# An adaptive layernorm and a mixture of eight experts on one core: the routing of a pair moved one slot back, its rows scattered one block per slot, and the first experts' bounds, rows and register reads moved forward

## What is computed

```python
z = relu(x @ Wd[ids] + bd[ids])                       # 256 -> 128, adapter of the sequence
y = x + z @ Wu[ids] + bu[ids]
y = layernorm(y) * g[ids] + b[ids]

probs = softmax(y @ gate_w + gate_b)                  # 8 experts
values, chosen = top_k(probs, k=2)
values = values / (sum(values) + 1e-9)
moe = sum over e of weight[e] * (gelu(y @ ew1[e] + eb1[e]) @ ew2[e] + eb2[e])
out = x + y + gelu(y @ sh_w1 + sh_b1) @ sh_w2 + sh_b2 + moe     # 256 -> 1024 -> 256
```

## Time and profile before

| | |
|---|---|
| runs of the kernel before | 699.71, 700.79, 702.68 us; median 700.79 |
| the profiled execution | 698.72 us, of which 697.0 is the span of the core's instructions |
| PE, DVE, ACT, POOL busy | 616.9, 510.9, 388.1, 386.5 us of the span |
| mean granted PE clock | 0.96 |
| phase one | to about 277.5 us |
| full expert tiles | 283.2 to about 633 us |
| half expert tiles and the end | 633 to 697 us |

### The profile page before, as it was taken

How to read it: one execution, slowest core, us unless ns; L and a number is a source line. 1 busy time by engine, 2 the same in 40 slices (tenths; PEclk the granted TensorE clock), 3 DMA queues, 4 the chain that set the end, 5 groups by cost and what they waited for, 6 DMA issues and landing times.

```text
span 697.0 us, 16951 instructions
## 1 busy us (share of the span) xinstructions
PE 616.9 (89%) x5073; PEld 491.0 (70%) x5073; DVE 510.9 (73%) x1198; ACT 388.1 (56%) x662; POOL 386.5 (55%) x320
## 2 busy tenths in 40 slices
PE   4465988887987898799999999999999999999894
PEld 2232655564654465688888888888888888888673
DVE  2859679575767567369898989889897776776652
ACT  1536655366375575457667666777664354354442
POOL 2434765657557441015666666575666766766534
PEclk9878999999999999899999999999999999999998
DMA  8754464636313364634756666655724424424310
GB/s 278 254 136 114 139 185 119 181 108 198 101 34 111 92 214 138 196 79 100 143 132 146 131 135 134 123 123 115 152 42 78 69 47 69 65 38 62 60 28 3
DMA packets 116742, 81.33 MB, mean 117 GB/s; under 512 B 71090, under 2 KB 106162, under 8 KB 116658
## 3 DMA queue, kind: packets, MB, share of 16 engines
q1 hardware_dynamic: 101346, 61.16, 34.7%
q0 software_dynamic: 13296, 16.92, 12.8%
q10 hardware_dynamic: 2016, 2.16, 1.0%
HBM read 43.21 MB, written 24.42 MB: 97 GB/s over the span
## 4 chain that ended last, share of the span: by engine, by line
PE 65%; DVE 10%; ACT 6%; DMA 6%; issue 5%; SPq 5%; another core or an unknown queue 2%; POOLq 0%; ACTq 0%; POOL 0%; DVEq 0%
PE H L1196 28%; PE Y L1212 26%; SPq L282 4%; PE H L1144 4%; DMA xT<-wreg 4%; PE Y L1156 3%; PE Z L1086 2%; ACT wreg L499 2%; DVE wreg L762 1%; DVE wreg L788 1%; ACT hf L552 1%; ACT hh L560 1%; DMA wreg<-in_wpack 1%; DVE wreg L731 1%
## 5 line engine op out<-in xcount | busy, mean ns | idle before, releaser
L1196 PE MATMUL H<-xT,wreg 128*128 128x256 f16 (+1 forms) x1872 | 206.9, 265 | 9.7 <-DMA xT<-xs_rows 5.7
L1196 PEld LDWEIGHTS H<-xT,wreg 128*128 x1872 | 173.9, 98 | 35.9 <-issue 12.1
L1212 PE MATMUL Y<-wreg,hh 128*128 x1136 | 188.3, 273 | 0.0
L1212 PE MATMUL Y<-wreg,hl 128*128 x568 | 154.8, 273 | 0.0
L601 ACT ACTIVATE hf<-H,prme 128x256 f32<-128x256 f32 (+1 forms) x312 | 145.7, 547 | 1.4 <-ACT prme L592 0.2
L1017 DVE SCALAR_TENSOR_TENSOR hl<-hf,prme,hh 128x512 f16<-128x512 f32 (+1 forms) x156 | 130.2, 835 | 5.5
L1015 DVE TENSOR_SCALAR hh<-hf,prme 128x512 f16<-128x512 f32 (+1 forms) x156 | 82.2, 527 | 70.0 <-ACT hf L601 69.3
L455 POOL TENSOR_SCALAR b2w<-b2t,wsel 128x256 f32<-128x256 f32 x71 | 79.2, 1252 | 87.7 <-DVE wsel L1032 87.7
L1212 PEld LDWEIGHTS Y<-wreg,hh 128*128 128x128 f16 x1136 | 111.1, 98 | 14.0
L1144 PE MATMUL H<-xT,wreg 128*128 128x512 f16 x384 | 99.5, 414 | 8.2 <-DMA xT<-wreg 7.8
L1156 PE MATMUL Y<-wreg,hh 128*128 128x256 f16 x512 | 85.6, 273 | 7.0 <-DVE hl L960 6.1
(11 more groups left out here) (189 smaller groups left out, 712.4 us busy)
## 6 DMA issues: line engine op xcount, KB each, us to landing
stage<-in_w SPq DMA_DIRECT2D x16, 1024.0 KB
b2t<-in_b SPq DMA_DIRECT2D x39, 128.0 KB
wreg<-in_wpack SPq DMA_DIRECT2D x16, 256.5 KB
wreg<-in_xt SPq DMA_DIRECT2D x16, 256.0 KB
wreg<-in_x SPq DMA_DIRECT2D x16, 256.0 KB, 5.6
wreg<-in_vecs SPq DMA_DIRECT2D x16, 256.0 KB, 3.5
out_y<-wreg SPq DMA_DIRECT2D x16, 256.0 KB
xs_rows<-wreg SPq DMA_DIRECT2D x9, 260.0 KB
```

Source lines behind the costliest of these rows:

```text
L1196: m = pe.matmul(H[c][:, half * w:(half + 1) * w], we[:, bass.ds(e + h * 2048 + k * 1024 + col, P)], xp[:, a + k, 0:w], start=i == 0, stop= ...
L1212: m = pe.matmul(Y[n % 2][:, j * D:(j + 1) * D], hx[:, n % 2, c * w + j * P:c * w + (j + 1) * P], we[:, bass.ds(e + 4096 + h * 2048 + c * D ...
```

## The change

The change touches the tables of slots, and the places of seven steps:

- `then(s, o)` is `at` with one slot more for pairs 0 to 5. `logits`, `choose`, `exps`, `rank`, `place` and `weigh` use it: offsets 8, 9, 9, 10, 11 and 11 in place of 7, 8, 8, 9, 10 and 10. Pairs 6 and 7 stay.
- `scatter(p, i)` of pairs 0 to 5 stands at the end of slot offset 11 + i, one block (two DMAs) per slot. For pairs 6 and 7 two blocks stand in slots 10 and 11 as before.
- The pads move from slot 26 to 28, and `load_rows(0)` and `(1)` from slot 30 to 29, ahead of the output stores of slot 30.
- The first expert's units: `unit_sums(3)` goes to slot 27, `unit_bound(2)` and `(3)` between `gemm1` and `gemm2` of slots 28 and 29, `unit_high` and `unit_low` of both one slot forward.
- PE reads `ready` and `slot` of tile 0 between slots 30 and 31, and those of tile n+1 between `expert_gemm1(n)` and `expert_gemm2(n-1)`. From tile 32 on `ready` is not read, and the wait is for all units.
- ACT reads its register and copies its parameters before it waits for PE; `first_bias(n)` stands in tile n itself, behind group 2.
- DVE's `select(n)` stands ahead of tile n's `split_h`.

```diff
+def then(s, o):
+    return [p for p in range(NP) if s - base(p) == o + (p < NP - 2)]
-START = [-6, -2, 27, 28]
+START = [-6, -2, 27, 27]
 # sync engine
+                if s == 29:
+                    sp.wait_ge(v_etab, 1)
+                    for n in range(2):
+                        load_rows(n)
-                if s == 26:
+                if s == 28:
                     sp.wait_ge(v_ptab, 1)
                     for e in range(NE):
                         pad(e)
-                if s == 27:
-                    sp.wait_ge(v_etab, 1)
-                if s == 30:
-                    for n in range(2):
-                        load_rows(n)
 # gpsimd
-                for p in at(s, 11):
-                    scatter(p, 2)
-                    scatter(p, 3)
...
-                for p in at(s, 10):
-                    scatter(p, 0)
-                    scatter(p, 1)
+                for p in range(NP):
+                    for i in range(4):
+                        if s == base(p) + (11 + i if p < NP - 2 else 10 + i // 2):
+                            scatter(p, i)
 # scalar
-                for p in at(s, 8):
+                for p in then(s, 8):
                     exps(p)
...
-                act.wait_ge(pe_h, 4 * n + c + 1)
                 if c == 0:
...
                     act.wait_ge(ae_prm, n + 1)
+                act.wait_ge(pe_h, 4 * n + c + 1)
...
-                    if c == 1 and n:
-                        first_bias(n - 1)
+                    if c == 2:
+                        first_bias(n)
...
-            first_bias(NX - 1)
 # vector
-                for p in at(s, 10):
+                for p in then(s, 10):
                     place(p)
                     weigh(p)
-                for p in at(s, 8):
+                for p in then(s, 8):
                     choose(p)
...
                 if s == 28:
                     tables()
+                    unit_low(2)
+                if s == 29:
+                    unit_low(3)
...
                 if n < NX:
+                    select(n)
                     for c in range(4):
                         split_h(n, c)
...
-                    select(n)
 # tensor
+                if s == 28:
+                    unit_bound(2)
+                if s == 29:
+                    unit_bound(3)
                 if s >= 4:
                     gemm2(t - 1, q)
-                for p in at(s, 9):
+                for p in then(s, 9):
                     rank(p)
-                for p in at(s, 7):
+                for p in then(s, 7):
                     logits(p)
...
+                if s == 30:
+                    pe.wait_ge(v_etab, 1)
+                    ready = pe.value_load(...)
+                    slot = pe.value_load(...)
...
                 if n < NX:
-                    ready = pe.value_load(...)
-                    slot = pe.value_load(...)
-                    pe.wait_ge(v_low, ready)
+                    now = slot
+                    if n < NF:
+                        pe.wait_ge(v_low, ready)
+                    else:
+                        pe.wait_ge(v_low, NU)
                     expert_gemm1(n, slot)
+                if n + 1 < NF:
+                    ready = pe.value_load(...)
+                if n + 1 < NX:
+                    slot = pe.value_load(...)
                 if n == 0:
                     for j in range(4):
                         gemm2(NP - 1, j)
                 else:
                     expert_gemm2(n - 1, before)
+                before = now
```

More of the change, by code:

```diff
@@ L577, in scalar_program @@
                     norm(p)
-                for u in early(s, 3 if s < 4 else 2):
-                    unit_high(u)
+                if s < 4:
+                    for u in early(s, 3):
+                        unit_high(u)
+                if s == 28:
+                    unit_high(2)
+                if s == 29:
+                    unit_high(3)
                 if s == FIRST + 1:
@@ L994, in vector_program @@
                     constants()
-                for u in early(s, 4 if s < 4 else 2):
-                    unit_low(u)
-                for u in early(s, 2 if s < 4 else 1):
-                    unit_scale(u)
+                if s < 4:
+                    for u in early(s, 4):
+                        unit_low(u)
+                if s < 4:
+                    for u in early(s, 2):
+                        unit_scale(u)
+                if s == 28:
+                    unit_scale(2)
+                if s == 29:
+                    unit_scale(3)
                 if s >= 0:
@@ L1178, in tensor_program @@
                     down(2 * p)
-                for u in early(s, 1):
-                    unit_bound(u)
+                if s < 4:
+                    for u in early(s, 1):
+                        unit_bound(u)
                 if s == 25:
                     total()
+                if s == 30:
+                    pe.wait_ge(v_etab, 1)
+                    ready = pe.value_load(etab[0:1, 3 * NX:3 * NX + 1], min_val=4, max_val=2 * NE + 2)
+                    slot = pe.value_load(etab[0:1, 2 * NX:2 * NX + 1], min_val=0, max_val=8192 * (NE - 1))
             def expert_gemm1(n, e):
@@ L1214, in expert_gemm2 @@
                 m.then_inc(pe_y, 1)
-            pe.wait_ge(v_etab, 1)
-            slot = None
             for n in range(NX + 1):
-                before = slot
                 if n < NX:
-                    ready = pe.value_load(etab[0:1, 3 * NX + n:3 * NX + n + 1], min_val=4, max_val=2 * NE + 2)
-                    slot = pe.value_load(etab[0:1, 2 * NX + n:2 * NX + n + 1], min_val=0, max_val=8192 * (NE - 1))
-                    pe.wait_ge(v_low, ready)
+                    now = slot
[3 more added lines that the diff above has]
+                        pe.wait_ge(v_low, NU)
                     expert_gemm1(n, slot)
+                if n + 1 < NF:
+                    ready = pe.value_load(etab[0:1, 3 * NX + n + 1:3 * NX + n + 2], min_val=4, max_val=2 * NE + 2)
+                if n + 1 < NX:
+                    slot = pe.value_load(etab[0:1, 2 * NX + n + 1:2 * NX + n + 2], min_val=0, max_val=8192 * (NE - 1))
                 if n == 0:
```

## The result

| | before | after |
|---|---|---|
| median (range) | 700.91 us (699.71 to 702.68) | 661.93 us (657.54 to 665.19) |
| ratio | | 0.944 [0.937, 0.951] |
| the profiled execution, its span | 698.72, 697.0 us | 665.19, 663.3 us |
| mean granted PE clock | 0.961 | 0.969 |

The four timed runs of the change spread over 7.6 us, those of before over 3.0, and the profiled one is the slowest of them.

The account below looks back on a forecast made before the run. PE was taken to bound the full tiles, so gains lie only in phase one, the change of phases, and half tiles and end: 10 + 4.4 + 5.9 + 1.2 = 21.5, forecast median 679.3 us, range 670 to 687.

Parts of the forecast that it names:

- Phase one: Slots before the change of phases: 60% of 12.3 us transpose waits plus 4.2 us slow clock, 10 us; bounds 0 and 24.
- I cost this relief at nothing, since PE's waits of the same slots are counted already: Phase one: shorter runs of POOL additions, which stall DVE, add 0; 7.8 + 4.3 us, less overlap, in the upper bound only.
- one slot more should cover all five: Phase one: logits one slot later hides PE's transpose waits of pairs 1 to 5, 12.3 us in all.
- The prediction's 4.2: Phase one: slow PE clock after transpose waits, 1.4 us each, seen behind three of five, 4.2 us.
- the runs of POOL were the true brake: Rival, chance 0.09: cutting POOL's runs frees DVE as well; phase one gives 24 us, in all 665.3 us.
- the upper bound: Phase one: at most 24 us gained; about 17 if a DVE instruction waits for only one POOL addition, by the skill's rule.
- The waits move: Rival, chance 0.18: PE waits for `place`, gelu or DVE instead, phase one keeps its length; 689.3 us.
- The last block comes late: Rival, chance 0.05, slower: in phase one ACT's `high_rows` waits for scatter block 3, PE behind it; 718 us.
- It doesn't do what it says: Rival, chance 0.04: later logits still meet unlanded rows and the reads still show; within 3 us of 700.79.
- Change of phases: Between phase one and the tiles: first tile starts 3.3 us earlier and runs 1.1 us shorter, 4.4 us; bounds 0 and 7.7.
- Half tiles and end: Last tiles: 5 x 1.18 = 5.9 us from PE's reads, and 1.2 us from the last outputs leaving earlier.
- one read, placed where the queue is full, keeps that: Half tiles: one register read doesn't show, so a tile takes 6.7 us instead of 7.88; 5.9 us, bounds 2 and 6.

Follow-up runs that it names:

- e11: The changed kernel run once more, nothing altered: 659.12 us, ratio 0.939.
- e2: Kernel before with only the scatter of pairs 0 to 5 spread, one block per slot, routing where it was: 683.91 us, ratio 0.975.
- e1: Kernel before with only the routing of pairs 0 to 5 one slot later, the eight scatter DMAs still in a row, also one slot later: 697.05 us, ratio 0.994.
- e13: The kernel before, unchanged, run again with a profile of its own: 701.73 us, ratio 1.000.
- e9: Kernel before with the routing one slot later and all eight scatter DMAs in one row at the end of slot offset 12: 685.87 us, ratio 0.980.
- e3: Kernel before with both phase-one parts, routing one slot later and one scatter block per slot, phase two as before: 669.58 us, ratio 0.955.
- e5: Changed kernel with pads, first row loads and first expert's units of the change of phases as before: 659.57 us, ratio 0.941.
- e6: Changed kernel with PE's two register reads where they were before, ahead of the matmuls: 660.92 us, ratio 0.945.
- e10: Changed kernel, but in the half tiles PE reads the next tile's slot inside `expert_gemm2`: 659.03 us, ratio 0.942.

## Why the prediction was wrong

**What bounds, right.** The full tiles hardly moved (345.9 us, and 347.3, 346.2 and 343.7 in the three profiles of the change), and all the gain lies in the three stretches named.

**Phase one, wrong in size and in cause: 10 us forecast, 30 measured** (69.5 + 128.1 + 56.6 against 63.9 + 107.6 + 52.4 in e11). The step that failed is "I cost this relief at nothing, since PE's waits of the same slots are counted already". The relief of POOL is the larger part: 17.8 us alone (e2) and 27.5 on top of the routing (697.05 to 669.58). The part that the term was built on, the routing, gives 4.7 alone and 14.3 on top of the relief. The reasoning took PE's wait for the transposes as something of its own. But the transposes hang on POOL: `rows` feeds `high_rows`, that feeds `low_rows`, and this the transposes; and `low_rows` stands on DVE behind whatever POOL's additions hold up, as in the chain of the kernel before. With the row in place a later `logits` only shows POOL's lateness one step earlier, as ACT's 32.4 us in e1; without the row the wait partly goes by itself, from 8.8 us between slots 4 and 20 before to 5.7 in e2. A second step failed in part: "one slot more should cover all five". For pairs 1 and 2 `gemm1` of slots 4 and 8 needs the same transposes, so 4.0 of the 12.3 us moved there.

The windows tell what the 20.5 us of slots 4 to 19 are: the kernel before as e13 has it, e2, e9 and e3.

```profile
68.40:197.90 129.50, 112.84 (x747) 75.05 (x746) 97.18 (x241) 70.08 (x91) 80.31 (x73) 0.93 0.49 143
```

```profile
68.50:184.20 115.70, 110.00 (x747) 74.23 (x746) 88.97 (x240) 73.34 (x96) 81.76 (x71) 0.95 0.54 154
```

```profile
63.80:189.50 125.70, 111.70 (x757) 75.12 (x758) 92.43 (x257) 72.92 (x97) 82.70 (x70) 0.93 0.49 141
```

```profile
63.90:171.60 107.70, 105.86 (x756) 73.06 (x757) 96.77 (x251) 71.30 (x95) 84.41 (x71) 0.98 0.63 168
```

From the first to the last, PE's idle time falls from 16.7 to 1.8 us and its busy time, for nearly the same count of matmuls (747 and 756), from 112.8 to 105.9, as the granted clock goes from 0.93 to 0.98. So some 7 of the 22 us came with the clock. The prediction's 4.2 for it, over all five waits, was of the right kind.

**The rival "the runs of POOL were the true brake", 665.3 with 0.09,** was the nearest, in time and in mechanism: additions that stall DVE are what the chain of the kernel before runs through. It is not the whole. Stalls are still there in the change (4.99 and 4.15 us), and e1, which has only short ones, is slow because the DMAs hold `rows`. Its time is also near by some luck, since it had 24 us for phase one, where 30 came, and 11.5 for the rest, where 8.3 came. How many us each of the two ways costs was not separated by a run.

**"The waits move"** is nearly what the routing alone does: in e1 it gives 4.7 us, where the rival has 0 (its 689.3 holds the 11.5 of the other parts, which e1 leaves out). The spreading takes most of it away. **"The last block comes late"** fell: ACT's waits for the landing do not appear, and with one block per slot phase one is at its fastest. **"It doesn't do what it says"** fell: phase one does what it says but for the waits of `gemm1` above.

**The Trainium skill** (SBUF — State Buffer, the rules on the shared port pair) has the second of the two instructions wait until the first finishes. A DVE instruction of 1.28 us waited through three additions (97.90 to 101.61) and one of 128 x 4 numbers through four instructions of POOL (91.43 to 95.24), so a run of them counts as one, as the prediction held against the page. Nor is it always the first to start that goes on: by the profile's starts the DVE instruction in the changed kernel is 0.18 and 0.56 us ahead of POOL's first addition (97.72 and 97.90, 104.30 and 104.86), and yet it is the one that waits. By the page the upper bound would have been 17 for phase one, and the 30 measured exceed even the trace's 24.

**Change of phases, nearly right:** for the start of tile 0 3.3 us were forecast and 3.0 measured from slot 28 on, though the three profiles of the change range from 26.0 to 27.8 us, against 29.1 and 29.2. The wait for the rows is gone (0.28 for 5.70 us) since no store stands between the last pad and the first rows. For the first tile 1.1 us were forecast, and it is 2.05 shorter. Its length goes with the wait ahead of it: 6.9 to 8.3 us behind waits of 2.9 to 5.7 us (nine profiles), 5.4 us behind at most 1.4 (nine profiles, e5 with the old order among them). In two of the three profiles of the change the full tiles lose this again, by gaps of 0.5 to 1.1 us in the next tiles.

**Half tiles and end, right in kind, the first too large: 7.1 forecast, 5.3 measured.** In the half tiles 1.18 us were to go five times; 0.58 went in each of the four periods from the third `expert_gemm1` on (7.88 to 7.30), 2.3 in all, and 2.0 in the two before them, so 4.3 for 5.9. The step "one read, placed where the queue is full, keeps that" failed: PE stood about 0.75 us a tile at the one read, the case for which the bound of 2 was named. e6 gives 4.4 us to the reads alone. The end was right: from the start of the last `expert_gemm1` to the first of the last two additions it took 686.85 - 677.76 = 9.1 us and now 653.15 - 645.17 = 8.0, and those two stand 3.60 us apart: 1.1 for 1.2.

**The signs.** Of those listed as right, the pads, the first tile close behind PE's last `gemm2` and the additions at the end came true. The waits for transposes came true for `logits` alone: behind the one that moved to `gemm1` in slot 4 the mean granted clock is 0.71 from 63.7 to 74.1 us. "No DVE instruction over 4 us" and "half tiles at 6.7 us without gaps" did not come true, and the gap before `gemm2` that was listed as wrong is there.

## What to carry to other kernels

An engine's queue in order is a resource: price a burst of cheap instructions by what stands behind it in that queue and by how its length compares with the period of the loop (11 us in a loop of 6.7), whatever its engine's busy share; and where a wait is on the chain behind such an engine, do not count it as the gain of moving the waiter. Read on the chain how the burst reaches the bound engine: in the kernel before it did so through DVE, although the burst was POOL's. Two edits on the same loop are priced together: here 4.7 and 17.8 made 32.1. Compare traces stretch by stretch between the same instructions, since the median of a kernel whose phases race can move by more than a small part is worth.

## What the runs showed of the hardware

An indirect DMA held POOL for 0.96 us in most cases (50 of 64 in the kernel before, the longest 1.9), with 0.30 between two, and this did not shrink in a row of eight. A DVE instruction of 1.28 us that met a run of POOL's additions ended about 1.1 us after the last of them, even where it had started first. A register read on PE left it idle for 0.65 to 0.90 us behind matmuls of 128 columns and mostly for 0.15 to 0.23 behind such of 256 columns, with loads of 0.30 to 0.52 us in both the change and e10; but a half tile became only 0.2 us shorter by it, and why is not shown. And the same kernel before took 701 us in five comparisons and 686 in one, where the spread of runs within each was under 7 us.
